# GpSimd's sends of expert outputs without their wait on gate products, in a decoder layer with mixture of experts

## What is computed

```python
x = x + _L0_attn_ref(_layernorm(x, axis=-1), ...)       # gated mixer
x = x + _L0_xattn_ref(_layernorm(x, axis=-1), ctx_1024, ...)  # 16 heads, relu features
x = x + _L0_ffn_ref(_layernorm(x, axis=-1), ...)
# _L0_ffn_ref
logits = xf @ router_w.T
routing = jax.nn.softmax(logits, axis=-1)
top_w, top_i = lax.top_k(routing, K)                    # K = 2
top_w = top_w / jnp.sum(top_w, axis=-1, keepdims=True)
g = jnp.einsum('nd,ehd->neh', xf, w_gate)
u = jnp.einsum('nd,ehd->neh', xf, w_up)
h = jax.nn.silu(g) * u
y = jnp.einsum('neh,edh->ned', h, w_down)
out = jnp.einsum('ned,ne->nd', y, combine)              # combine: top_w at top_i
```

## Time and profile before

| | us |
|---|---|
| median of 3 runs | 298.99 (297.98 to 299.67) |
| profiled execution, its own time | 297.59 |
| its span, first to last instruction | 295.8 |
| TensorE busy in the span | 255.7 (86%) |
| VectorE, ScalarE busy | 186.1 (63%), 161.9 (55%) |
| GpSimd busy | 124.4 (42%) |
| 39 sends, busy on GpSimd | 38.1, 0.978 each |
| 32 scatters, busy on GpSimd | 31.2, 0.976 each |
| expert stage, first gate product to last yo | 200.81 to 281.21 |
| mean granted TensorE clock | 0.972 |

### The profile page before, as it was taken

One profiled execution on the slowest core, in us unless ns is written; L12 is line 12 of the kernel. 1 busy time (PEld: TensorE's weight loads), 2 busy tenths in 40 slices (PEclk: granted clock), 3 DMA queues, 4 the chain that ended last, 5 costly groups with the idle time before them and its releaser, 6 DMA issues.

```text
span 295.8 us, 5756 instructions
## 1 busy us (share of the span) xinstructions
PE 255.7 (86%) x1697; PEld 215.9 (73%) x1697; DVE 186.1 (63%) x713; ACT 161.9 (55%) x343; POOL 124.4 (42%) x183
## 2 busy tenths in 40 slices
PE   6999999999999999999899979967979788779700
PEld 3848677677788998998699868956869687768600
DVE  3777768596869888895989788877752121122206
ACT  1656465565687777675767576634635344335400
POOL 5638999651010001016401640633566556565520
PEclk9999999999999999999999999999999979999955
DMA  6999999970040000001000100147875887662148
GB/s 194 283 213 179 188 188 177 179 86 2 1 142 2 0 2 1 1 2 54 21 0 0 47 29 2 49 139 196 237 213 156 263 244 212 179 181 74 40 148 279
DMA packets 38446, 34.05 MB, mean 115 GB/s; under 512 B 3581, under 2 KB 31234, under 8 KB 38288
## 3 DMA queue, kind: packets, MB, share of 16 engines
q1 hardware_dynamic: 35312, 28.96, 44.2%
q0 software_dynamic: 2272, 4.24, 4.1%
q10 hardware_dynamic: 832, 0.49, 0.7%
HBM read 19.80 MB, written 14.32 MB: 115 GB/s over the span
## 4 chain that ended last, share of the span: by engine, by line
PE 65%; DVE 11%; issue 8%; DMA 6%; POOL 6%; ACT 1%; another core or an unknown queue 1%; SPq 1%; ACTq 0%; POOLq 0%; DVEq 0%
PE num L1310 15%; PE bank L1397 8%; PE num L1407 6%; PE bank L1271 5%; PE num L1249 5%; PE bank L246 4%; PE bank L248 4%; PE bank L247 4%; DVE X L945 3%; PE num L246 2%; PE bank L1213 2%; PE num L248 2%; PE num L247 2%; DMA X<-in_x 2%; PE bank L1173 2%
## 5 line engine op out<-in xcount | busy, mean ns | idle before, releaser
L945 DVE SCALAR_TENSOR_TENSOR X<-num,rden,X 128x128 f32<-128x128 f32 x256 | 75.8, 342 | 4.7
L1310 PEld LDWEIGHTS num<-kvw_sb,q 128*128 128x128 f32 x512 | 66.6, 190 | 13.7 <-issue 5.7
L1310 PE MATMUL num<-kvw_sb,q 128*128 128x130 f32 x512 | 69.3, 277 | 5.2 <-DVE X L945 4.2
L547 POOL DMA_INDIRECT dispatched<-rows,slot_i x32 | 31.2, 976 | 57.3 <-PE bank L248 30.1
L682 ACT ACTIVATE relu_z<-bank 128x512 f32<-128x512 f32 x64 | 38.0, 594 | 23.0 <-PE bank L248 21.0
L582 POOL DMA_INDIRECT expert_out<-yo,xb x39 | 38.1, 978 | 27.8 <-ACT yo L714 16.4
L1133 DVE TENSOR_TENSOR hid<-bank,silu_g 128x256 f32<-128x256 f32 x39 | 16.5, 423 | 51.9 <-ACT silu_g L710 32.7
L1397 PE MATMUL bank<-xT,wgu_sb 128*128 128x128 f32 x312 | 42.8, 282 | 4.4 <-issue 3.5
L599 ACT ACTIVATE q<-relu_z 128x512 f32<-128x512 f32 x64 | 40.4, 632 | 6.7 <-DVE acc L860 0.8
L1397 PEld LDWEIGHTS bank<-xT,wgu_sb 128*128 128x128 f32 x312 | 39.0, 196 | 5.4 <-issue 5.4
L1407 PE MATMUL num<-wd_sb,hid 128*128 x156 | 26.1, 291 | 6.8 <-DVE hid L1133 4.6
(11 more groups left out here) (173 smaller groups left out, 396.2 us busy)
## 6 DMA issues: line engine op xcount, KB each, us to landing
wgu_sb<-in_wgu SPq DMA_DIRECT2D x39, 256.0 KB
dispatched<-pad_row SPq DMA_DIRECT2D x3, 2795.0 KB, 35.9
xb<-dispatched SPq DMA_DIRECT2D x39, 65.0 KB
y_back<-expert_out SPq DMA_DIRECT2D x4, 512.0 KB, 4.7
wd_sb<-in_wd SPq DMA_DIRECT2D x1, 1024.0 KB, 4.8
out<-X SPq DMA_DIRECT2D x4, 256.0 KB, 2.5
X<-in_x SPq DMA_DIRECT2D x3, 256.0 KB, 6.7
expert_out<-yo,xb POOLq DMA_INDIRECT x39
```

What stands on the lines that cost most here:

```text
L547: g.indirect_dma_start(out=xs, out_offset=bass.IndirectOffsetOnAxis(ap=slot_i[:, m % 2, t, k:k + 1], axis=0), in_=rows[:, m % 2, k, t, :], ...
L945: ins = v.scalar_tensor_tensor(tile_of(n, t), banks[:, t // 2, t % 2, 0:P], rden[:, f % 2, t:t + 1], tile_of(n, t), ALU.mult, ALU.add)
L1310: last = nc.tensor.matmul(num[:, 2 * (h % 2) + t // 2, HA * (t % 2):HA * (t % 2 + 1)], q[:, h % 4, part], kvw_h, start=True, stop=True)
```

## The change

The wait on `gu_full` in front of sends 4 to 38 is taken out. The wait on `yo_done` stays, and so do the waits of the last scatters on gate products.

```diff
             def send(s, j, turn):
-                if s >= BURST:
-                    pool.wait_ge(gu_full, BURST_GATES[-1] + 1 + (s - BURST) * (RUN - 1 - BURST_GATES[-1]) // (RUN - BURST))
                 wait_alone(pool, yo_done, s + 1)
                 g.indirect_dma_start(
```

## The result

| | before, us | after, us |
|---|---|---|
| median, same chip, 20 executions each | 299.36 (297.09 to 301.59) | 301.28 (299.11 to 304.71) |
| ratio, 95% interval | | 1.0077 (1.0047 to 1.0106) |
| profiled execution / its span | 297.59 / 295.8 | 302.64 / 300.8 |
| last send issued | 282.04 | 286.76 |
| mean granted TensorE clock | 0.972 | 0.954 |

The changed kernel is slower by 0.8%, some 2 us, where 2.7 us faster was forecast. The interval lies clear of 1, and 0.5% falls just inside its lower end: a small loss, but a loss. The two profiled executions lie 5.0 us apart, more than the medians, so about 3 us of what the traces show is the spread of single executions.

A forecast was written before the change was run, and what follows sets the result against it. Halts of TensorE and ScalarE beside unbroken GpSimd DMA runs were taken to bound the expert stage. Gains of 4.4 (cheap) and 1.1 us (dear) gave 2.7 between: 298.99 - 2.7 = 296.3 us, range 292.0 to 303.8.

The forecast's parts named there:

- the halts: Expert stage: engines wait for one another beside GpSimd's DMA runs; blocks 13 to 32 lose 13.3 us, the last 1.7.
- No change: Rival, 299.0 us: each send costs about 0.43 us wherever it goes, or halts don't come from GpSimd; chance 0.28.
- the sends as passengers: Rival case counted with no change, expert stage: halts don't come from GpSimd at all, so the time stays the same.
- the tail: End of the expert stage: last sends already follow their tiles by 0.83 us, so the direct gain is 0.
- First part: Expert stage, sends catching up from send 4: between no gain by gate product 22 and gate product 16 only at 238.
- the dear bound: Catch-up: one halt through sends 4 to 12, gate product 16 at 238; with 1.76 a block, 1.1 us earlier.
- The clock: TensorE's clock in the expert stage: a longer halt can bring the 1.2 GHz fall once more, 1.2 us worse.
- the middle: Gate product 38: 2.7 us earlier, taken between the cheap first part's 4.4 and the dear one's 1.1.
- The cheap bound: Catch-up: halts cost what they did before, gate product 22 at 245.28 as now; with 1.76 a block, 4.4 us earlier.
- Second part: Expert stage after catch-up: each send goes 0.83 us after its tile, with blocks at 1.76 us each.
- the 1.81 that decides: Expert stage: from 238 before needed 1.81 us for each of the 22 blocks left, the point where *Slower* decides.
- Slower: Rival, 303.8 us: the unbroken run holds TensorE through catch-up, then blocks take 2.03 us, costing 4.8; chance 0.30.

The follow-up runs named there:

- the probes: Kernel before plus GpSimd DMAs, plain DMAs or memsets in batch 0's quiet attention; ten GpSimd DMAs back to back 308.49 us against 300.52, one a head 298.85 against 301.43.
- the spaced sends: Kernel before with the wait drawn closer, one send per gate product: 298.98 us against 300.52, ratio 0.9961.
- the probe beside which nothing else changed: Kernel before plus ten back-to-back GpSimd DMAs of padding in batch 0's quiet attention: 308.49 us against 300.52, one execution.
- the second set: Runs on one chip with the kernel before at 300.52 us; the changed kernel repeated there took 302.39 us, ratio 1.0049.
- the last set: Runs with the kernel before at 281.39 us; the changed kernel plus ten plain SyncE DMAs and 12 GpSimd memsets took 280.89 us, ratio 0.9992.
- the third: Set of runs with the kernel before at 301.43 us; waits taken from sends 4 to 12 alone gave 308.0 us, ratio 1.0199.
- the harmless probes: Ten plain SyncE DMAs and 12 GpSimd memsets in batch 0's attention, added to the changed kernel: 280.89 us against 281.39 for the kernel before, ratio 0.9992.

## Why the prediction was wrong

**What bounds the kernel, and the cause of the halts: right.** I read that GpSimd's runs of DMAs make the waits; the probes and the spaced sends bear it out. *No change* by a price per send is refuted by the spacing. So is the sends as passengers, where there are holds. The Trainium skill, SBUF — State Buffer, section "SBUF: two separate sides", by which engines and DMAs don't contend, gave 299.0; the probe beside which nothing else changed runs against reading it so in the second set (heads of 4.16 and 5.73 us), and the last set agrees with it (ratio 0.9992). No run shows that a port was contended for.

**The waits removed are free and held much back; nothing is gained at the tail: right.** Send 4 was set at 225.72 and came at 226.75, 1.26 us after the start of the last scatter as reckoned, which was itself 1.03 us later. SyncE gained nothing that shows: its waits on gate products ahead of weight loads are 7.3 us in 8 times instead of 4.8 in 6. (The row left out 3.9 us in 3 times that the same query of before puts down to remote; after has none.) At the tail nothing is gained; the last send came 1.15 us after its tile instead of 0.83, because send 37 went out just before it.

**First part: here it failed.** The run of sends 4 to 12 without rest came as the dear bound had it. It held the others not once but twice, with gate product 15 between the holds, and the second lasted beyond its end. The bound had TensorE at gate product 16 at 238, and it was at 242.24. The 4.2 us are, to about a tenth: 0.8 by which the run ended later (237.97 against 237.15); 1.1 by which the hold outlasted the run (1.87 against 0.8, the value of the short runs in the earlier trace rows); and 2.4 from the silu at 239.84 through `hid`, down product and turn to the gate product, where I had nothing, all at 1.2 GHz. I had the end of the silu's wait stand for the start of TensorE's next product. In the second set the same point stood at 243.25, in the third, with the first nine waits removed, at 243.43. The clock was priced at 1.2 us once more at worst; it stayed low for 13.7 us instead of 3.4.

**Taking the middle.** I had said that no row put the first part nearer to either end, and took 2.7 us of gain between 4.4 and 1.1. A run of nine where no run was longer than five was itself such a row: the mechanism that I had argued for, rest, leads to the dear end. The cheap bound needed halts that ignore the run's length, which is rival *No change*'s account and not the forecast's.

**Second part: right, with some luck.** From gate product 16 to 38 it took 39.5 us for 22 blocks, 1.80 each, just under the 1.81 that decides. This includes the end of the low clock; from number 18 on it is 34.78 / 20 = 1.74, against 1.76 taken and 2.03 in *Slower*. The wait on tiles alone doesn't secure this pace: with the same wait on sends 19 to 38, the kernel that kept the earlier ones took 2.18 from gate product 22 to 38, where this one took 27.42 / 16 = 1.71. Put together with the measured 242.24, 22 x 1.76 = 38.7 gives gate product 38 at 281.0, where it was 281.74. One number of the sum was wrong, and it alone turned the sign: 276.7 became 281.0, from 1.1 us earlier than before's 277.82 to 3.1 later.

**The rivals.** *Slower* had the right place and the right first half, and the wrong second: its 303.8 came from slow blocks afterwards, which did not come. The measured 301.28 lies between it and no change, and inside the range.

## What to carry to other kernels

A wait that looks like needless order can be what breaks a queue of indirect DMAs into short runs. Before taking it out, count how many instructions will then go out back to back, and price the run as one hold up to its end, with the restart of the chain behind it and a colder TensorE. The better change here is a closer wait, one send per gate product or nearly so, which was 0.4 to 0.5% faster than before where there are holds. It has its price where there are none, where it wasn't run: there gate product 38 came at 261.19 and the last send at 265.38, and with the 12.9 us that the one-per-gate kernel needed from the one to the other the last send would be at 274.1, an estimate of 8.7 us lost.

## What the runs showed of the hardware

- The same kernel took 299 to 301 us in some sets of runs and 281 in others, 6% apart. The difference lies where GpSimd issues indirect DMAs in runs. The changed kernel, with holds and (with the harmless probes) without: first relu of the attention at 80.08 and 80.04 us, the 33rd at 133.62 and 133.65, by when the first scatters have hardly begun, the last at 193.84 and 189.67, gate product 38 at 281.74 and 261.19. No trace of the 281 us sets has a hold, beside runs of 16 sends and more too. A null result in one set would have misled.
- Ten indirect DMAs of GpSimd 1.27 us apart stretched two heads to 4.16 and 5.73 us; 1.60 us apart they cost nothing (one execution each).
- The longest holds, 3.5 to 5.4 us, are put down to "remote" by the profile, not to the engine waited for, which had long been done.
- From the end of TensorE's idle time behind the first hold (2.81 us) the granted clock stayed at 1.2 GHz for 13.7 us, through the second. It was 13.7 us again in the repeat of the changed kernel and in the one with only the first nine waits taken out.
- A memset of 128x64 with a wait for it, 0.17 us of work, raised the pitch of the sends from 1.27 to 1.91 us.
